# Layer 1's dense products as three fp32r products instead of one fp32 product, and layer 2's softmax reciprocals turned at full width

## What is computed

```
# layer 1, per batch; zt_prev, za are 256 x 512
q = layer_norm((zt_prev + pos).T);  kv = layer_norm((za + pos).T)
Q = split(q @ Wq);  K = split(kv @ Wk);  V = split(kv @ Wv)
ctx = softmax(Q K^T / sqrt(16)) V
r = ctx @ Wo + q
h = layer_norm(r)
out = (gelu(h @ W1 + b1) @ W2 + b2 + r).T            # W1 256 x 512, W2 512 x 256
...
# layer 2, per batch: self attention, then cross attention, each with probabilities
# divided by the row sums of exp; then
out = x + gelu(layernorm(x) @ w1 + b1) @ w2 + b2     # w1 512 x 2048
```

## Time and profile before

| | |
|---|---|
| device time, median of 3 runs | 1847.55 us (1846.65 to 1848.02) |
| the profiled execution's own time | 1848.91 us |
| its span in the trace | 1847.1 us |
| PE busy over the span | 1727.9 us, 94% |
| DVE, ACT busy | 1203.1 us (65%), 1062.6 us (58%) |
| POOL busy | 99.5 us |
| mean granted PE clock | 0.963 of full |

### The profile page before, as it was taken

How to read it: one execution, slowest core, us unless ns; L and a number is a source line. 1 busy time by engine, 2 the same in 40 slices (tenths; PEclk the granted TensorE clock), 3 DMA queues, 4 the chain that set the end, 5 groups by cost and what they waited for, 6 DMA issues and landing times.

```text
span 1847.1 us, 34084 instructions
## 1 busy us (share of the span) xinstructions
PE 1727.9 (94%) x12736; PEld 1239.9 (67%) x12736; DVE 1203.1 (65%) x2792; ACT 1062.6 (58%) x2333; POOL 99.5 (5%) x79
## 2 busy tenths in 40 slices
PE   4879999999999988999999999999999889999999
PEld 2324343443434334788888788888888779999998
DVE  5666776767676552588878887888878753333332
ACT  2345666756666564687888777877777631111111
POOL 2110101101000000000000000000000000000000
PEclk7779999999999898999999999999999999999999
DMA  6322223223222222666557756666666340000000
GB/s 161 114 85 64 93 86 101 72 88 94 76 70 74 73 61 87 170 150 172 150 154 194 196 169 189 174 174 167 174 170 163 106 134 23 24 24 27 27 26 15
DMA packets 169485, 201.72 MB, mean 109 GB/s; under 512 B 25957, under 2 KB 117221, under 8 KB 169321
## 3 DMA queue, kind: packets, MB, share of 16 engines
q1 hardware_dynamic: 169032, 199.14, 38.4%
q10 hardware_dynamic: 288, 0.39, 0.1%
HBM read 131.84 MB, written 67.63 MB: 108 GB/s over the span
## 4 chain that ended last, share of the span: by engine, by line
PE 81%; DVE 9%; ACT 5%; issue 2%; DMA 1%; DVEq 1%; ACTq 0%; POOL 0%; SPq 0%
PE c_d L2097 10%; PE c_sums L2112 9%; PE b_d L1359 9%; PE b_d L1371 9%; PE a_d L499 6%; PE b_d L1438 5%; PE a_escore L472 5%; PE a_d L569 3%; PE a_d L577 3%; PE a_mscore L484 3%; PE b_score L1426 3%; PE a_d L553 3%; PE b_d L1455 3%; DVE a_mx L802 2%; PE a_d L561 2%
## 5 line engine op out<-in xcount | busy, mean ns | idle before, releaser
L802 DVE TENSOR_REDUCE a_mx<-a_mscore 128x2 f32<-128x1024 f32 x247 | 302.2, 1224 | 171.5 <-PE a_mscore L484 170.3
L639 ACT ACTIVATE a_pt<-a_escore 128x1024 f32<-128x1024 f32 x256 | 262.6, 1026 | 164.9 <-PE a_escore L472 164.7
L1588 ACT ACTIVATE b_pr<-b_t,b_nmax 128x256 f32<-128x256 f32 x512 | 254.4, 501 | 124.3 <-DVE b_nmax L1764 124.3
L1760 DVE TENSOR_TENSOR b_t<-b_score,b_mask 128x1024 f32<-128x1024 f32 x128 | 155.1, 1212 | 85.9 <-PE b_score L1426 85.5
L2196 ACT ACTIVATE c_gT<-c_d,c_b 128x256 f32<-128x256 f32 x128 | 53.9, 473 | 266.1 <-PE c_d L2097 266.0
L1764 DVE CUSTOM_DVE_ANT_0 b_t<-b_t,b_minus 128x256 f32<-128x256 f32 x512 | 187.3, 421 | 16.9
L472 PEld LDWEIGHTS a_escore<-a_qst,a_kst 50*128 50x128 f32 x512 | 50.0, 191 | 180.3 <-ACT a_pt L639 110.4
L472 PE MATMUL a_escore<-a_qst,a_kst 50*128 50x512 f32 x512 | 133.9, 519 | 24.1 <-ACT a_pt L639 23.4
L2241 DVE CAST c_g_high<-c_gT 128x512 fp32r<-128x512 f32 x64 | 40.2, 628 | 171.0 <-ACT c_gT L2196 171.0
L2097 PE MATMUL c_d<-c_ln_high,c_w_high 128*128 128x256 f32 x512 | 144.7, 283 | 2.3 <-DVE c_ln_low L2243 2.3
L2097 PE MATMUL c_d<-c_ln_high,c_w_low 128*128 128x256 f32 x512 | 144.9, 283 | 0.0
(11 more groups left out here) (165 smaller groups left out, 3233.1 us busy)
## 6 DMA issues: line engine op xcount, KB each, us to landing
b_qst<-b_q SPq DMA_DIRECT2D x96, 256.0 KB, 4.8
b_kst<-b_k SPq DMA_DIRECT2D x96, 256.0 KB, 6.4
b_q<-b_qparts SPq DMA_DIRECT2D x64, 256.0 KB, 5.1
b_k<-b_kparts SPq DMA_DIRECT2D x64, 256.0 KB, 3.6
a_qst<-a_q_parts SPq DMA_DIRECT2D x192, 64.0 KB, 2.2
a_kst<-a_k_parts SPq DMA_DIRECT2D x186, 64.0 KB, 2.2
a_k_parts<-a_kparts SPq DMA_DIRECT2D x32, 256.0 KB, 2.3
a_q_parts<-a_qparts SPq DMA_DIRECT2D x32, 256.0 KB, 2.3
```

Of the source, the lines that this page charges most:

```text
L639: nc.scalar.activation(pt[:, at % RING, :, :], escore[:], ACT.Exp, scale=SCALE).then_inc(exp_done.sem, 1)
L802: nc.vector.tensor_reduce(mx[:, 2 * pair:2 * pair + 2, q], maxima_bank(b, n)[:], AX_X, ALU.max).then_inc(max_done.sem, 1)
L1588: last = nc.scalar.activation(pr[:, u % 2, j, :], t[:, u % 2, j, :], ACT.Exp, scale=-1.0, bias=nmax[:, u, j:j + 1], accum_out=esum[:, u, j ...
```

## The change

**Part a.** Each dense weight is held as two fp32r tiles (high, low), split once at the start: ACT writes the high part, DVE the low part. The raw weights are loaded into the room of `pt`. Each dense product becomes three fp32r products (`products`). The operands that move are split too: `kvn` by POOL (`split_context`), the normalised queries, the hidden state and the GELU result by ACT (high) and DVE (low), the context out of PSUM. Queries, context, hidden state and the low half of the GELU result take turns in one tile `pair`. GELU becomes two instructions of 1024 columns and moves behind the second exponential of position 8 and behind `keep_context`; before, it stood ahead of that exponential. The k and q products that stood between positions 8 and 9 on PE are elsewhere: k in position 6, q in position 15. The fetch of the next inputs moves to the end of a round. **Part b.** POOL spreads the reciprocals over 128 columns (`widen`), PE turns each unit with one 128 x 128 transpose. The bias rows use all 128 partitions, and weight 1 is loaded into `stage` too, after weight 0 has been split.

```diff
-        wo = sb("wo", [P, CT, C])
-        w1 = sb("w1", [P, CT, F])
-        w2 = sb("w2", [P, FT, C])
+        wo = sb("wo", [P, 2, CT, C], F32R)
+        w1 = sb("w1", [P, 2, CT, F], F32R)
+        w2 = sb("w2", [P, 2, FT, C], F32R)
...
         STEPS = {
             0: ["E0", "M0", ("m", 0, 1), ("pv", -1, 3, 0), ("pv", -1, 3, 1), "E1", "M1", ("pv", -1, 3, 2), ("pv", -1, 3, 3)],
-            1: ["E0", "M0", ("v", 0, 0, 0), ("v", 0, 0, 1), "E1", "M1", ("ctx", -1, 3), ("v", 0, 1, 0)],
-            2: ["E0", "M0", ("v", 0, 1, 1), ("ctxT", -1), "E1", "M1", ("y", -1, 0, 0), ("y", -1, 0, 1)],
+            1: ["E0", "M0", ("v", 0, 0, 0), ("ctx", -1, 3), "E1", "M1", ("v", 0, 0, 1), ("ctxT", -1)],
+            2: ["E0", "M0", ("v", 0, 1, 0), ("v", 0, 1, 1), "E1", "M1", ("y", -1, 0, 0), ("y", -1, 0, 1)],
             3: ["E0", "M0", ("y", -1, 1, 0), ("y", -1, 1, 1), "E1", "M1", ("tok", 2, 0), ("tok", -1, 2)],
             4: ["E0", "M0", ("m", 0, 2), ("pv", 0, 0, 0), ("pv", 0, 0, 1), "E1", "M1", ("pv", 0, 0, 2), ("pv", 0, 0, 3)],
-            5: ["E0", "M0", ("ctx", 0, 0), ("tok", 2, 1), "E1", "M1", ("chan", -1, 2)],
-            6: ["E0", "M0", ("f1", -1, 0, 0), ("f1", -1, 0, 1), "E1", "M1", ("f1", -1, 1, 0), ("f1", -1, 1, 1)],
-            7: ["E0", "M0", ("f1", -1, 2, 0), ("f1", -1, 2, 1), "E1", "M1", ("f1", -1, 3, 0), ("f1", -1, 3, 1)],
+            5: ["E0", "M0", ("ctx", 0, 0), ("chan", -1, 2), "E1", "M1", ("tok", 2, 1)],
+            6: ["E0", "M0", ("k", 1, 1, 0), ("k", 1, 1, 1), "E1", "M1", ("f1", -1, 0, 0), ("f1", -1, 0, 1)],
+            7: ["E0", "M0", ("f1", -1, 1, 0), ("f1", -1, 1, 1), ("f1", -1, 2, 0), "E1", "M1", ("f1", -1, 2, 1), ("f1", -1, 3, 0), ("f1", -1, 3, 1)],
             8: ["E0", "M0", ("m", 0, 3), ("pv", 0, 1, 0), ("pv", 0, 1, 1), "E1", "M1", ("pv", 0, 1, 2), ("pv", 0, 1, 3)],
-            9: [("k", 1, 1, 0), ("k", 1, 1, 1), ("q", 1, 1, 0), "E0", "M0", ("q", 1, 1, 1), ("ctx", 0, 1), "E1", "M1", ("f2", -1, 0, 0)],
-            10: ["E0", "M0", ("f2", -1, 0, 1), ("f2", -1, 0, 2), "E1", "M1", ("f2", -1, 0, 3)],
+            9: ["E0", "M0", ("ctx", 0, 1), "E1", "M1", ("chan", 2, 1)],
+            10: ["E0", "M0", ("f2", -1, 0, 0), ("f2", -1, 0, 1), "E1", "M1", ("f2", -1, 0, 2), ("f2", -1, 0, 3)],
             11: ["E0", "M0", ("f2", -1, 1, 0), ("f2", -1, 1, 1), "E1", "M1", ("f2", -1, 1, 2), ("f2", -1, 1, 3)],
             12: ["E0", "M0", ("m", 1, 0), ("pv", 0, 2, 0), ("pv", 0, 2, 1), "E1", "M1", ("pv", 0, 2, 2), ("pv", 0, 2, 3)],
-            13: ["E0", "M0", ("chan", 2, 1), "E1", "M1", ("ctx", 0, 2), ("chan", 2, 0)],
-            14: ["E0", "M0", ("k", 2, 0, 0), "E1", "M1", ("k", 2, 0, 1)],
-            15: ["E0", "M0", ("q", 2, 0, 0), "E1", "M1", ("q", 2, 0, 1)],
+            13: ["E0", "M0", ("ctx", 0, 2), ("chan", 2, 0), "E1", "M1", ("k", 2, 0, 0)],
+            14: ["E0", "M0", ("k", 2, 0, 1), "E1", "M1", ("q", 2, 0, 0)],
+            15: ["E0", "M0", ("q", 2, 0, 1), ("q", 2, 1, 0), "E1", "M1", ("q", 2, 1, 1)],
         }
...
+            def split_context(b):
+                if not there(b):
+                    return
+                v_filled.need(pool, b - 2, 2)
+                chan_done[1].need(pool, b, CT)
+                nc.gpsimd.tensor_copy(kvp[b % 2][:, 0], room(b, 1)).then_inc(kvn_high.sem, 1)
+                kvn_high.need(pool, b, 1)
...
+            def products(at, w, src, steps, k):
+
+                for n, (x, y) in enumerate(PRODUCTS):
+                    mm = nc.tensor.matmul(at, w(x), src(y), start=(k == 0 and n == 0), stop=(k == steps - 1 and n == 2))
+                return mm
...
+            def high_weight(n):
+                if n == 0:
+                    act.wait_ge(qkv_in.sem, 16 * QKV)
+                elif n == QKV:
+                    act.wait_ge(late_in.sem, 16 * LATE)
+                nc.scalar.activation(WEIGHTS[n][1][:, 0], staged(n), ACT.Copy).then_inc(w_high.sem, 1)
...
             def gelu(b):
                 if not there(b):
                     return
-                act.wait_ge(f1_raw.sem, f1_raw.at(b, FT))
-                nc.scalar.activation(gT[:], gT[:], ACT.Gelu).then_inc(g_done.sem, 1)
+                for h in range(2):
+                    act.wait_ge(f1_raw.sem, f1_raw.at(b, 2 * h + 2))
+                    nc.scalar.activation(gT[:, 2 * h:2 * h + 2, :], gT[:, 2 * h:2 * h + 2, :], ACT.Gelu).then_inc(g_done.sem, 1)
+
+            def high_gelu(b, h):
+                if not there(b):
+                    return
+                f2_filled.need(act, b - 1, CT)
+                g_done.need(act, b, h + 1)
+                nc.scalar.activation(gh[:, 2 * h:2 * h + 2, :], gT[:, 2 * h:2 * h + 2, :], ACT.Copy).then_inc(g_high.sem, 1)
 
...
             def position(i, p):
+                if p == 2:
+                    context(i - 1)
+                    if i == FIRST + 1:
+                        for n in range(QKV, len(WEIGHTS)):
+                            high_weight(n)
                 exponentials(*unit_of_exp(i, p, 0))
                 if p == 0:
                     negative_maxima(i, 1)
+                    high_part(i + 1, 0, 1)
+                if p == 4:
+                    negative_maxima(i, 2)
+                if p == 5:
+                    to_channels(i - 1, 2)
+                if p == 6:
+                    keep_tokens(i + 2, 1)
+                if p == 7:
+                    keep_up(i - 1, 0)
+                if p == 8:
+                    negative_maxima(i, 3)
+                    keep_up(i - 1, 2)
+                    keep_up(i - 1, 3)
+                    if i == FIRST:
+                        for n in range(QKV):
+                            high_weight(n)
+                if p == 9:
+                    high_gelu(i - 1, 0)
+                if p == 10:
+                    to_channels(i + 2, 1)
+                if p == 12:
+                    negative_maxima(i + 1, 0)
+                if p == 13:
+                    to_channels(i + 2, 0)
+                exponentials(*unit_of_exp(i, p, 1))
+                if p == 0:
+                    keep_context(i - 1, 3)
                 if p == 1:
                     values(i, 0)
                 if p == 2:
                     values(i, 1)
-                    context(i - 1)
-                if p == 4:
-                    negative_maxima(i, 2)
-                if p == 6:
-                    keep_up(i - 1, 0)
-                if p == 7:
-                    keep_up(i - 1, 2)
-                if p == 8:
-                    negative_maxima(i, 3)
-                    gelu(i - 1)
-                if p == 12:
-                    negative_maxima(i + 1, 0)
-                if p == 9:
-                    high_part(i + 1, 1, 1)
-                if p == 13:
-                    to_channels(i + 2, 1)
-                exponentials(*unit_of_exp(i, p, 1))
-                if p == 0:
-                    keep_context(i - 1, 3)
                 if p == 3:
                     keep_tokens(i + 2, 0)
                     keep_tokens(i - 1, 2)
                 if p == 4:
                     keep_context(i, 0)
                 if p == 5:
-                    keep_tokens(i + 2, 1)
-                    to_channels(i - 1, 2)
+                    high_hidden(i - 1)
                 if p == 6:
+                    high_part(i + 1, 1, 1)
+                if p == 7:
                     keep_up(i - 1, 1)
-                if p == 7:
-                    keep_up(i - 1, 3)
                 if p == 8:
                     keep_context(i, 1)
+                    gelu(i - 1)
                 if p == 9:
-                    high_part(i + 1, 0, 1)
+                    high_gelu(i - 1, 1)
                 if p == 12:
                     keep_context(i, 2)
                 if p == 13:
-                    to_channels(i + 2, 0)
+                    high_queries(i + 2)
                 if p == 14:
                     high_part(i + 2, 1, 0)
                 if p == 15:
...
+            def low_context(b):
+                if not there(b):
+                    return
+                for c in range(CT):
+                    ctx_high.need(dve, b, c + 1)
+                    nc.vector.tensor_tensor(pair[:, 1, c, :], bank("ctxT", b, c), pair[:, 0, c, :].bitcast(F32),
+                                            ALU.subtract).then_inc(ctx_low.sem, 1)
+
+            def low_hidden(b):
+                if not there(b):
+                    return
+                h_high.need(dve, b, 1)
+                nc.vector.tensor_tensor(pair[:, 1], hT, pair[:, 0].bitcast(F32), ALU.subtract).then_inc(h_low.sem, 1)
...
             def position(i, p):
                 row_maximum(*unit_of_max(i, p, 0))
+                if p == 0:
+                    low_part(i + 1, 0, 1)
+                if p == 1:
+                    divide_context(i - 1, 3)
+                if p == 2:
+                    low_context(i - 1)
                 if p == 3:
                     residual_sum(i - 1, 1)
+                    if i == FIRST + 1:
```

(30 more changed lines are left out.)

309 lines of the change are left out of this document (212 added, 97 removed).

## The result

The changed kernel takes 1897.16 us (median of 4 runs, 1895.81 to 1899.52), the kernel before beside it 1847.78: ratio 1.0269, interval 1.0254 to 1.0284. It is slower by 49 us; I had forecast 7 slower and a range of 1833 to 1876, so the measurement lies 21 us above the range.

The account below looks back on a forecast made before the run. Parts a and b were taken as bound by PE. Opening +5, rounds 1 to 5 +7, round 6 +2, clock +11 and part b -18 sum to +7, forecasting 1855 us; own range 1846 to 1868, range of all 1833 to 1876.

Parts of the forecast that it names:

- Opening: Start of part a: POOL's split of kvn and stacking behind three parts delay the first products; +5 us (2 to 8).
- The GELU wait: Part a, position 9: PE waits about 5.1 us for ACT in each round with a GELU.
- Dense products: Part a: three fp32r products save 0.24 us per product, 32 x 0.24 = 7.7 us less PE time per round.
- PE's other work: Part a: PE's work without waits in a round, 76.8 us before with 3.2 us of waits, falling to 69.1.
- Other waits: Part a, positions 6 to 15 and context transposes: new waits beside the GELU's, 7.2 us a round.
- rival 2: Part a faster: half of the 7.2 us of other waits falls away, queues being empty; 1833 us, chance 0.22.
- The clock: Part a: half-speed work behind the GELU wait, +1.8 to +2 us a round, 11 us for six rounds.
- The passage: From part a's last rounds into part b: round 7 at 0, round 8 likewise 0.
- Part b: Part b: reciprocals by full transposes, 64 pairs x 0.35 us = 22 less; taken as -18 us (-12 to -22).
- (1): Rival: the clock holds in rounds 1 to 6 despite the GELU wait; 1844 us, chance 0.17.
- (3): Rival, slower by more: POOL late or contending with DVE, opening +8, part b's gain only 12; 1876 us, chance 0.11.
- (4): Rival: dense products save what waits cost, part b's gain pays for the opening; 1847 us, chance 0.08.

Follow-up runs that it names:

- experiment 3: Changed kernel with the first layer's GELU and its two table loads left out (a probe): 1858.18 us, ratio 1.0054 to the kernel before.
- experiment 4: Control: the kernel before with its first-layer GELU and table loads left out (a probe): 1845.14 us, ratio 0.9983.
- experiment 12: Changed kernel with the table loads kept and the GELU cut to one column of each tile (a probe): 1883.56 us, ratio 1.0197.
- Experiment 5: Changed kernel; in the passage the last batch's f1 copies, GELU and splits queue ahead of part b's steps on ACT and DVE: 1878.00 us, ratio 1.0172.
- experiment 6: Experiment 5's kernel with part b's two weight splits in round 7 behind positions 10 and 14 instead of 8 and 12: 1878.43 us, ratio 1.0168.
- experiment 9: The kernel before with widened reciprocals and the bias row and ones over 128 partitions instead of 64: 1841.56 us, ratio 0.9964.
- experiment 13: Kernel 9 with DVE doing the low part of the encoded input ahead of the second residual sum: 1828.77 us, ratio 0.9901 to the kernel before.
- experiment 14: Experiment 13's kernel with the subtraction for the encoded low part also cut to four columns (a probe): 1826.64 us, ratio 0.9889.
- experiment 15: The kernel before with the encoded low part first and its subtraction cut, without widening and full-width bias (a probe): 1839.66 us, ratio 0.9962.
- experiment 16: Experiment 3's kernel with only the high-by-high product of each three in the first layer's dense products (a probe): 1867.32 us, ratio 1.0111 to the kernel before.
- kernel 1: The kernel before with only the second layer's widening of the reciprocals and full transpose: 1844.42 us, ratio 0.9983.
- both cures: Changed kernel with Experiment 5's queue order in the passage and the encoded low part ahead of the second residual sum: 1870.68 us, ratio 1.0124.
- experiment 7: Changed kernel with k products moved from position 6 to 9 to cover the GELU, with the steps belonging to them: 1906.21 us, ratio 1.0318.
- experiment 10: The kernel before with only the bias row and ones over 128 partitions instead of 64: 1844.27 us, ratio 0.9983.

## Why the prediction was wrong

- **Opening: right.** POOL's cast (1.41 us there) and subtraction (2.35) put the first k product from 20.56 to 24.80 us, and the first M stands at 41.49 (37.18 before); I had said 42. My term was +5; up to round 0 it was +3.2.
- **The GELU wait: right.** 4.99 us in every round from 1 to 6, against 5.1. Experiments 3, 4 and 12 show that ACT's block is its cause and that the old order hid it.
- **Dense products: mis-sized, the first step that failed.** I took 0.24 us less for each of 32, 7.7 a round. Distances between starts, summed over a round, give 31.2 us before and 26.1 (q 3.6, k 3.5, v 3.3, y 3.2, f1 and f2 12.5): 5.1 less. Six products take 1.56 us and nine 2.30, so each group pays 0.13 to 0.16 us more than its 0.238 a product in the long stream of the earlier trace rows gives, and the fp32 groups paid nothing of the kind. Three products cost 0.78 (f1, f2) to 0.90 us (q) rather than 0.715. The term "32 x 0.24" is wrong by 2.6 us a round, 15 us in six rounds; this is read from the traces, and no run took the groups apart.
- **PE's other work** I had read as 76.8 us; summed in the same way it is 78.6 before, with 1.5 us of waits and not 3.2. So the new round holds 74.1 us of work at full clock where I had 69.1: 1.8 of the 5.0 from this start, 2.6 from the dense products, the rest in small lengthenings of transposes, E and M.
- **Other waits: too large, and this hid most of it.** I had 7.2 beside the GELU; the round has 3.5 (M of position 7 1.15 for my 1.3; an E of position 6 0.76 for 0.45; f1 0.2 for 0.45; q 0.6 and halves of 13 to 15 0.7 for 2.3; M of position 10 none). That is rival 2's reason, an engine held at the GELU leaves empty queues behind it, and experiment 3 shows it: without the GELU the wait of position 10 appears at 1.05 us.
- **The clock: about right,** 1.2 to 2.5 us a round for my 1.8 to 2. Together a full round takes 84.0 to 85.2 us; I had 83.2. That it came so near was luck, two errors of opposite sign: 5.0 us too little work and 3.8 us too much waiting.
- **The passage: the step that failed most.** The prediction put round 7 at 0 and "Round 8 likewise 0"; together they became +26.6 us. I had followed the new order through a full round and not through rounds 7 and 8, where part b's own steps stand in the same ACT and DVE queues. Experiment 5 takes 19 us off the kernel by order alone, 16.3 of them in this stretch. What is left there, 10.3 us over the kernel before, stands beside 13.0 us more of waits: the E of position 9 behind the GELU and the weight split 6.9 us (2.7 and 2.0 in two places before), y for the low part of the context 3.6 (nothing before), f1 for the low part of the hidden state 3.9 (0.5 before). Apart from the weight split in experiment 6, no run took these one by one.
- **Part b: -18 became about -8.** Three things. A pair saves 0.24 us and not 0.35, because the change from narrow to full products, 0.11 us dearer than staying narrow, only moved ahead of the reciprocals. The bias edit, costed at nothing, brings as much again. And in the cross rounds, which I had not looked at ("the stretches that I looked at have no gap"), PE waits 1.89 us per round for DVE, and 2.06 in the changed kernel; experiments 9 and 13 to 15 show that this wait and the half clock behind it take the saving. In the later cross rounds of the changed kernel this leaves 0.1 us a round.
- **The rivals.** (1), a clock that holds, did not come: it fell in each of rounds 1 to 6. (3), slower by more, had the sign and 1876 us, but not the reasons: no wait of PE in a full round names POOL, the opening cost less and not more, and only its smaller gain of part b (12 for 8 measured) pointed the right way. (4), no change, did not come.

In sum I had the sign and the mechanism of part a's rounds (+20 forecast for rounds 0 to 6, +26 measured), and missed 27 us in the passage, 10 in part b and 6 in the rounds.

The Trainium skill (TensorE: Matmul & The Clock Gate, Why this matters for your kernels) puts the return to the low clock down to idle pauses. The 4.99 us wait agrees. Experiment 16 is nearer to another section of that page (A second HAM failure mode: psum-queue depth-cycling), which tells of short idles between groups of matmuls that let the clock swing: in the trace of experiment 16 the longest wait in the round is 2.07 us, and the granted clock 0.81.

**Open.** Why the same 2.06 us wait lowers the clock in one cross round and not in the next, or in kernel 9 and not in kernel 1, these runs don't settle. Nor is it settled what lowers the clock in experiment 16: one of its waits, their number, or the smaller share of work in the round. Of the 42 us that the first layer's change costs with both cures in place, only the GELU block's part is shown by a run (experiment 3); the rest is read from the traces.

## What to carry to other kernels

Follow a new order of queues through every stage that shares them, not only through the steady round: the expensive place was where the last batch of one part met the first of the next. Before cheaper work of an engine is booked as a gain, find the wait of that round and shorten it first: here one swapped line, on top of the two edits of part b, was worth 12.8 us, twice what they had brought; on the kernel before alone it was not run. Work moved to fill a wait must come from where nothing waits: in experiment 7 new waits came up in the position it left and behind the one it filled.

## What the runs showed of the hardware

- Less work can be slower: with 15 us less of products in a round (experiment 16 against 3) PE was granted 0.81 of its clock instead of 1.00, and the stretch took 83.4 us instead of 79.3.
- A ones-by-bias product over 128 partitions among full products was cheaper than one over 64: 0.38 us less in the place shown, and a self round of part b 0.5 us shorter (experiment 10).
- A change between full products and narrow ones (32 columns of the array) costs time of its own: starts stand 0.20 us apart there, 0.09 between groups of narrow ones and 0.11 between full transposes (kernel before, 941 to 943 us).
- In the changed kernel GpSimd's cast of 128 x 1024 takes 1.08 us, its subtraction 2.38, the widening of four reciprocals to 128 x 128 0.33 (means; 1.41 and 2.35 in the opening); in the full rounds no wait of PE names them.
